# Two gated cross-attention blocks on one core: the first block's mixture moved to TensorE, and several pieces of work put elsewhere in the engines' orders

## The reference

```python
x = x + tanh(g_xattn[0]) * wkv(w, u, k=layernorm(x), v=ctx)
x = x + tanh(g_ffn[0])   * ffn(layernorm(x), w_gate_up, w_proj)
x = x + tanh(g_xattn[1]) * attention(layernorm(x), ctx, mask)
x = x + tanh(g_ffn[1])   * fp8_linear(layernorm(x), weight, bias)

# wkv: two scans over the 64 tokens of each batch row with the decay exp(w):
#   sums of exp(k) * v and of exp(k); y = (sum + exp(u+k) v) / (sum + exp(u+k))
# ffn: gate, up = x @ q(w_gate_up).T; h = silu(gate) * up; rms_norm(h) @ q(w_proj).T
#   q: each group of 64 weights becomes -s, 0 or +s, s the mean magnitude of the group
# fp8_linear: one scale from the greatest |x| of the whole tensor, x rounded to fp8
```

## Time and profile before

| | us |
|---|---|
| median of 3 runs (lowest, highest) | 138.73 (138.19, 139.01) |
| profiled execution | 137.42 |
| its span | 135.6 |
| mean granted TensorE clock of the span | 0.962 |
| TensorE busy | 115.7 |
| VectorE busy | 112.8 |
| ScalarE busy | 90.6 |
| GpSimd busy | 34.9 |

### The profile page before, as it was taken

One profiled execution on the slowest core, in us unless ns is written; L12 is line 12 of the kernel. 1 busy time (PEld: TensorE's weight loads), 2 busy tenths in 40 slices (PEclk: granted clock), 3 DMA queues, 4 the chain that ended last, 5 costly groups with the idle time before them and its releaser, 6 DMA issues.

```text
span 135.6 us, 2220 instructions
## 1 busy us (share of the span) xinstructions
PE 115.7 (85%) x729; PEld 76.4 (56%) x739; DVE 112.8 (83%) x265; ACT 90.6 (67%) x188; POOL 34.9 (26%) x79
## 2 busy tenths in 40 slices
PE   5958799960999799999987999999997768899991
PEld 5846674410523356477653676766666546677680
DVE  5999999998995979999986896938898897882970
ACT  2487789039584877685775777895975555864962
POOL 7917100006000000000134712019537432620000
PEclk9999999997557999999999999999999999999999
DMA  4999970000000000000000000000000000000035
GB/s 122 272 346 352 381 214 2 0 0 0 0 0 0 0 5 2 0 0 0 0 0 5 2 0 0 0 5 0 0 2 0 5 0 2 0 2 0 5 116 193
DMA packets 7110, 6.90 MB, mean 51 GB/s; under 512 B 1336, under 2 KB 6842, under 8 KB 7098
## 3 DMA queue, kind: packets, MB, share of 16 engines
q1 hardware_dynamic: 7088, 6.75, 15.7%
q10 hardware_dynamic: 10, 0.00, 0.0%
HBM read 5.70 MB, written 1.05 MB: 50 GB/s over the span
## 4 chain that ended last, share of the span: by engine, by line
PE 52%; DVE 16%; ACT 14%; DMA 7%; SPq 5%; issue 5%; DVEq 0%
PE ps L850 8%; PE ps L851 7%; DMA wgu_raw<-in_L_ffn_w_gate_up_dram 7%; PE ps L909 5%; DVE xs L1216 4%; PE ps L883 4%; PE ps L1103 4%; DVE stats L1127 3%; PE ps L770 3%; PE ps L772 3%; ACT xn L521 2%; PE ps L815 2%; ACT wT L527 2%; PE ps L752 2%; PE ps L841 2%
## 5 line engine op out<-in xcount | busy, mean ns | idle before, releaser
L850 PE MATMUL ps<-wT,xhi 128*128 128x512 bf16 x60 | 23.8, 396 | 1.3 <-ACT xlo L544 1.0
L851 PE MATMUL ps<-wT,xlo 128*128 128x512 bf16 x60 | 23.4, 390 | 0.2
L909 PE MATMUL ps<-wT,wgu_raw 128*128 128x256 bf16 x128 | 16.6, 273 | 0.1
L417 POOL TENSOR_SCALAR ve<-mv 128x2 f32<-128x2 f32 (+2 forms) x10 | 2.5, 246 | 52.8 <-DVE mv L1133 52.8
L909 PEld LDWEIGHTS ps<-wT,wgu_raw 128*128 128x128 f16 x128 | 12.4, 98 | 1.6 <-DVE wgu_raw L1283 0.3
L1127 DVE BATCH_NORM_STATS2 stats<-xs 128x6 f32<-128x256 f32 x32 | 12.3, 413 | 1.1 <-DMA xs<-in_x_dram 0.8
L585 ACT ACTIVATE wgu_raw<-ps 128x512 f16<-128x512 f32 x16 | 9.5, 595 | 4.5 <-PE ps L883 4.0
L533 ACT ACTIVATE wscale<-ps 128x1024 bf16<-128x1024 f32 x6 | 6.1, 1023 | 8.4 <-PE ps L772 8.4
L850 PEld LDWEIGHTS ps<-wT,xhi 128*128 128x128 f16 x64 | 6.4, 100 | 7.7 <-ACT xlo L544 1.5
L851 PEld LDWEIGHTS ps<-wT,xlo 128*128 128x128 f16 x64 | 6.5, 101 | 7.3 <-issue 1.1
L883 PE MATMUL ps<-ident,hbuf 128*128 128x128 f32 x64 | 9.7, 275 | 0.9 <-DVE wgu_raw L1283 0.9
(11 more groups left out here) (172 smaller groups left out, 282.8 us busy)
## 6 DMA issues: line engine op xcount, KB each, us to landing
wgu_raw<-in_L_ffn_w_gate_up_dram SPq DMA_DIRECT2D x4, 512.0 KB, 8.9
ctx_sb<-in_ctx_dram SPq DMA_DIRECT2D x2, 512.0 KB, 7.4
wp_raw<-in_L_ffn_w_proj_dram SPq DMA_DIRECT2D x1, 1024.0 KB, 10.1
out_dram<-xs SPq DMA_DIRECT2D x3, 256.0 KB, 2.1
xs<-in_x_dram SPq DMA_DIRECT2D x2, 256.0 KB, 3.0
xs<-in_x_dram SPq DMA_DIRECT2D x1, 512.0 KB, 6.9
wlin_raw<-in_L_ffn_weight_dram SPq DMA_DIRECT2D x1, 256.0 KB, 9.0
out_dram<-xs SPq DMA_DIRECT2D x2, 128.0 KB, 1.9
```

Of the source, the lines that this page charges most:

```text
L850: pe.matmul(ps[:, bank, :], xhi[:, h, c, o:o + P], w, start=(c == 0), stop=False)
L851: mm = pe.matmul(ps[:, bank, :], xlo[:, h, c, o:o + P], w, start=False, stop=(c == CH - 1))
L909: mm = pe.matmul(proj_at(i), part[:, n % 2, j * P:(j + 1) * P], wT[:, GU_PAIRS + f, j * C:(j + 1) * C], start=(first and f == 0 and j == 0 ...
```

## The change: what it does

- The first half's mixture is formed in PSUM: `mix_x` multiplies x with the identity into banks 0 and 1 (in place of six warm-up matmuls), `mix_y` adds y times tanh(g) times the identity (`ident_tg`, made by ScalarE at the start). ScalarE copies the banks to `res` (`mix_in`). `y_back(0)` and `mix_out` go.
- Variance plus epsilon and the shift of the first half are formed on VectorE, the root stays on GpSimd. ScalarE normalises all four tiles.
- GpSimd forms the two products of the second half (k = 2, 3) ahead of that root, after den_bonus(2). VectorE no longer does.
- `weight_rest` alternates between banks 6, 7 and 4, 5, so that (0) and (1) wait for no eviction. (0) to (3) are issued before the transposes, (4) in unit 0 and not in unit 1.
- gate(0) waits for the first low part alone; up(0) also for `gmax_done`, since the spread of the scales uses bank 1.
- VectorE's units: numerator scans 2 and 3 both in unit 3; bonus(3), both outputs and the quantisation of pair 5 in unit 4.
- project(6) is issued ahead of gate(8). The last unit's `hbuf` is turned in bank 1.
- Tail: `residual_back(2)` ahead of the third transposes, `spread_greatest` ahead of the last ones, no warm-up before it and two in place of four after it, `residual_back(4)` after the linear's block 1.
- The memset of `group_spread` goes from GpSimd to VectorE.

```diff
-WARM_LAST = 6
-WARM_TURN = 4
+WARM_TURN = 2
+    REST_BANK = [6, 4, 6, 4, 6, 6]
+        def turned(n):
+            return ps[:, 1 if n == UNITS - 1 else 3, :]
 # GpSimd
-            pool.memset(group_spread[:, :, :], 0.0).then_inc(spread_0, 1)
+            def wkv_product(k):
+                v = ctxT[:, k % CH, CT:NTOK].rearrange("p (b t) -> p b t", t=T)
+                pool.wait_ge(ctxT_ready, k + 1)
+                pool.wait_ge(G_ready, k + 1)
+                pool.tensor_tensor(kv[:, k, 1, :, 1:T + 1], kv[:, k, 0, :, 1:T + 1], v, ALU.mult).then_inc(GV_ready, 1)
             power(0, TPC, TPC, 2)
-            power_and_shift(1, 0, TPC, 1)
+            pool.wait_ge(den_ready, 3)
+            wkv_product(2)
+            wkv_product(3)
+            pool.wait_ge(ve_ready, 1)
+            pool.tensor_tensor(rstd[:, 1, 0:TPC], ve[:, 1, 0:TPC], minus_half[:, 0:TPC], ALU.pow).then_inc(rstd_ready[1], 1)
 # ScalarE
+            act.activation(ident_tg[:, :], ident[:, :], ACT.Copy, scale=tg[:, 0:1]).then_inc(ident_tg_ready, 1)
+            def mix_in(b):
+                act.wait_ge(mix_ps, b + 1)
+                act.activation(res[:, 2 * b:2 * b + 2, :]..., ps[:, b, :], ACT.Copy).then_inc(mix_ready, 1)
             invert(1)
+            mix_in(0)
+            mix_in(1)
+            invert(2)
             rest_in(0)
             rest_in(1)
-            invert(2)
-            ln_apply(1, 0, TPC // 2, 1)
+            act.wait_ge(mix_ready, 2)
+            ln_apply(1, 0, 2, 1)
+            ln_apply(1, 2, 2, 1)
 # TensorE
             def weight_rest(n):
-                    pe.wait_ge(rest_ready, n)
+                if n >= 2:
+                    pe.wait_ge(rest_ready, (0, 0, 1, 2, 3, 5)[n])
+            def mix_x():
+                pe.wait_ge(in_x[0], 16)
+                pe.wait_ge(in_x[1], 16)
+                pe.wait_ge(G_ready, CHUNKS * CH)
+                for i in range(TPC):
+                    o = (i % 2) * C
+                    pe.matmul(ps[:, i // 2, o:o + C], ident[:, :], xs[:, i, :], start=(i % 2 == 0), stop=False,
+                              skip_group_check=True)
+            def mix_y():
+                pe.wait_ge(y_ready, CH)
+                pe.wait_ge(ident_tg_ready, 1)
+                for i in range(TPC):
+                    for c in range(CH):
+                        o = (i % 2) * C + c * P
+                        mm = pe.matmul(ps[:, i // 2, o:o + P], y[:, c, i * P:(i + 1) * P], ident_tg[:, :], start=False,
+                                       stop=(i % 2 == 1 and c == CH - 1), skip_group_check=True)
+                    if i % 2:
+                        mm.then_inc(mix_ps, 1)
             def gate(n):
                 if n == 0:
-                    pe.wait_ge(G_ready, CHUNKS * CH)
+                    pe.wait_ge(mix_ready, 2)
+                    pe.wait_ge(mv_ready[1], 1)
+                    pe.wait_ge(xlo_ready, 1)
+                    pe.wait_ge(wq_ready, WQ_GATE[0])
+                if n == 2:
                     pe.wait_ge(xlo_ready, 2)
-                    pe.wait_ge(wq_ready, WQ_GATE[0])
             def up(n):
                 if n == 0:
                     pe.wait_ge(wq_ready, WQ_UP[0])
+                    pe.wait_ge(gmax_done, 1)
             def h_back(n):
-                if n >= 1:
+                if 1 <= n < UNITS - 1:
                     pe.wait_ge(hlo_ready, n)
-            keep_warm(WARM_FRONT, 0, wabs)
+            mix_x()
             for p in range(PAIRS):
                 weight_sums(p)
-            y_back(0)
-            weight_rest(0)
-            weight_rest(1)
+            mix_y()
+            for n in range(4):
+                weight_rest(n)
             spread_scales()
...
-            weight_rest(2)
             for n in range(UNITS + 2):
+                if n == 2 * TPC:
+                    project(n - 2)
                 if n < UNITS:
                     gate(n)
                     up(n)
...
                 if n == 0:
-                    weight_rest(3)
-                if n == 1:
                     weight_rest(4)
...
             channel_major(3, 1, xn3T_ps)
+            residual_back(2)
             channel_major(3, 2, xn3T_ps)
-            residual_back(2)
             channel_major(3, 3, xn3T_ps)
-            keep_warm(WARM_LAST, 7, wT)
+            spread_greatest()
             channel_major(3, 4, xn3T_ps)
-            spread_greatest()
             residual_back(3)
-            residual_back(4)
             keep_warm(WARM_TURN, 4, wT)
 # in the linear's loop, after block k
+                if k == 1:
+                    residual_back(4)
 # VectorE
+            dve.memset(group_spread[:, :, :], 0.0).then_inc(spread_0, 1)
             den_scan(2)
             weights_scale()
-            mix_out()
-            ln_stats(1, 0, TPC)
             den_bonus(2)
+            mix_stats()
             greatest_scales()
-            ln_apply(1, TPC // 2, TPC // 2, 1)
+            norm_shift()
             den_scan(3)
...
                 if n == 3:
-                    wkv_product(2)
-                    wkv_product(3)
                     num_scan(2)
+                    num_scan(3)
                     num_bonus(2)
+                if n == 4:
+                    num_bonus(3)
                     wkv_out(2)
-                if n == 4:
-                    num_scan(3)
-                    num_bonus(3)
                     wkv_out(3)
-                if n == 5:
                     quant_here(5)
                     quant_sign(5)
+                if n == 5:
                     mix_pair(2)
                     ln_stats(1, 4, 2)
```

More of the change, by code:

```diff
@@ L100, in gated_blocks @@
         neg_bf = sb("neg_bf", [P, P], BF16)
+        ident_tg = sb("ident_tg", [P, P])
         scales = sb("scales", [SCALE_ROWS, 512], BF16)
@@ L531, in rest_in @@
                 p = QUANT_ORDER[n]
+                bank = REST_BANK[n]
                 act.wait_ge(rest_ps, n + 1)
-                act.activation(wscale[:, p, :].rearrange("p (a b) -> p a b", a=2), ps[:, 6:8, :],
+                act.activation(wscale[:, p, :].rearrange("p (a b) -> p a b", a=2), ps[:, bank:bank + 2, :],
                                ACT.Copy).then_inc(rest_ready, 1)
+            def mix_in(b):
+                act.wait_ge(mix_ps, b + 1)
+                act.activation(res[:, 2 * b:2 * b + 2, :].rearrange("p i c -> p (i c)"), ps[:, b, :], ACT.Copy).then_inc(mix_ready, 1)
             def xn_high(k):
@@ L768, in weight_rest @@
                 for a in range(2):
-                    bank = 6 + a
+                    bank = REST_BANK[n] + a
                     pe.matmul(ps[:, bank, :], group_spread[:, SCALE_ROW[p] // 2 + a, :], scales[:, :],
@@ L894, in project @@
                 if n == 0:
-                    pe.wait_ge(gmax_done, 1)
+                    pe.wait_ge(rest_ready, 4)
                     pe.wait_ge(wT_ready, PAIRS)
@@ L1048, in _ @@
                     h_back(n - 1)
-                if n >= 2:
+                if n >= 2 and n != 2 * TPC:
                     project(n - 2)
@@ L1220, in residual, with mix_stats, norm_shift @@
                 dve.wait_ge(res_ready[stage], count)
-            def mix_out():
-                dve.wait_ge(tg_ready, 1)
-                dve.wait_ge(yT_ready, 2)
-                residual(1, 0, TPC, lambda i: ps[:, XN_BANKS[0][i // 2], (i % 2) * C:(i % 2 + 1) * C], lambda i: tg[:, 0:1], 1)
+            def mix_stats():
+                last = None
+                for i in range(TPC):
+                    if i % 2 == 0:
+                        dve.wait_ge(mix_ready, i // 2 + 1)
+                    now = step(dve.bn_stats(stats[:, i, :], res[:, i, :]))
+                    if i > 0:
+                        after(last)
+                        step(dve.bn_aggr(mv[:, 1, i - 1, :], stats[:, i - 1, :]))
+                    last = now
+                after(last)
+                dve.bn_aggr(mv[:, 1, TPC - 1, :], stats[:, TPC - 1, :]).then_inc(mv_ready[1], 1)
+                dve.wait_ge(mv_ready[1], 1)
+                dve.tensor_scalar(ve[:, 1, 0:TPC], mv[:, 1, 0:TPC, 1], LN_EPS, 1.0, ALU.add, ALU.mult).then_inc(ve_ready, 1)
+            def norm_shift():
+                dve.wait_ge(rstd_ready[1], 1)
+                dve.scalar_tensor_tensor(out=shift[:, 0:TPC], in0=mv[:, 1, 0:TPC, 0], scalar=-1.0, in1=rstd[:, 1, 0:TPC],
+                                         op0=ALU.mult, op1=ALU.mult).then_inc(shift_ready, 1)
             def mix_pair(k):
-                dve.wait_ge(yT_ready, k + 1)
-                residual(1, 2 * k, 2, lambda i: ps[:, XN_BANKS[1][k - 2], i * C:(i + 1) * C], lambda i: tg[:, 0:1], k)
+                dve.wait_ge(yT_ready, k - 1)
+                residual(1, 2 * k, 2, lambda i: ps[:, XN_BANKS[1][k - 2], i * C:(i + 1) * C], lambda i: tg[:, 0:1], k - 1)
             def weights_abs(p):
```

38 lines of the change are left out of this document (19 added, 19 removed).

## The result

| | median (lowest, highest), us | ratio to before, 95% interval |
|---|---|---|
| before, same chip | 138.66 (138.19, 139.01) | |
| after, first runs | 135.5 (134.14, 138.28) | 0.9692 [0.9635, 0.9749] |
| after, once more ("again") | 134.89 (134.11, 137.38) | 0.9717 [0.9693, 0.9741] |

What follows compares the result with a forecast made beforehand. No engine bounds the whole span; a chain of waits in four stretches does. Terms 2.7 - 1.7 + 0.5 + 0.55 + 0.6 = 2.65 us off the median 138.73 give 136.1 us, range 133.8 to 138.8.

Steps and rivals of the forecast that it cites:

- up to `ffn_in(2)`, low clock taken off: From the start to ffn_in(2): 2.7 us gained at full clock, 1.7 lost to a low spell, 1.0 left.
- project(6) ahead of gate(8): Unit 8: project(6) fills TensorE's 0.96 us wait for the low copy of x; 0.5 us gained.
- h_back(15) in bank 1: Start of the tail: the last h no longer waits for hlo(14); 0.55 us gained.
- the tail's end: Last linear: the greatest value's spread goes 1.4 us earlier, but TensorE's queue lets only 0.6 us arrive.
- VectorE's units 3 to 5: Pair 5's quantisation in unit 4 delays the sixth hbuf to 61.05, hidden by TensorE's queue; uncovered, up to 2.7 us.
- The front: Start, before ScalarE's exponentials: moved group_spread memset and new ident_tg copy cost 0, bounds -0.3 to +0.6 us.
- The first silu: Chain ahead of the loop: silu(0) starts at 39.35 us instead of 40.99, set by ScalarE's own queue.
- The clock: Low spell moves later, into the loop's start; a third of it, 3.4 us, is taken, costing 1.7 us.
- Long products: Rival: GpSimd's two products run long, VectorE's quantisations come 2.3 us late; 1.5 us more, 137.6. Chance 0.14.
- Chain not shortened: Rival: mix_y's weight loads or ScalarE's longer queue keep the first silu at 41; 138.8 us. Chance 0.11.
- The long spell in the dense loop: Rival: low clock starts at 41.9 and lasts 10.24 us in the loop; 0.75 us slower, 139.5. Chance 0.13.
- No spell: Rival: no low clock in the loop, so 4.35 us is gained; 134.4 us. Chance 0.22.

Runs made afterwards that it cites:

- old_tail: The changed kernel with the old tail, its old warm-up matmuls and the last h back in bank 3: 135.74 us, ratio 0.9808.
- f_proj: fill with project(6) back behind gate(8): 131.86 us, ratio 0.955.
- prod_dve: The changed kernel with the second half's two products back on VectorE in unit 3: 135.36 us, ratio 0.9707.
- fill: pad with eight unread matmuls of 512 columns between gate(0) and up(0): 132.69 us, ratio 0.9589.
- f_wr4: fill with weight_rest(4) back in unit 1: 131.64 us, ratio 0.952.
- old_units: fill with VectorE's old order in units 3 to 5, products still on GpSimd: 132.64 us, ratio 0.9613.
- no_mix: fill without the first half's mixture on TensorE; VectorE adds y to the residual in four instructions: 133.35 us, ratio 0.9646.
- pad: The changed kernel with the operands of the weight sums and of the scales' spread zero-padded from 24 to 128: 133.27 us, ratio 0.9591.
- best: fill with project(6) behind gate(8), weight_rest(4) in unit 1 and residual_back(4) ahead of the linear, replacing two unread matmuls: 130.35 us, ratio 0.9446.

## Why the prediction was right, and where its sum was not

**Direction and place: right.** The chain to the first silu got shorter, the gain reached the end, part of it went into a low clock inside the loop. That the sum came so near is in part luck: several of its terms were off, and they pull both ways. In "again" that spell lay at 41.5 to 44.9, 3.4 us long, in the end of `weight_rest(4)` and in gate(1) and up(1), inside the stretch of 38 to 46 that was forecast.

**The terms**, profiled executions, us gained:

| term | forecast | "again" against before |
|---|---|---|
| up to `ffn_in(2)`, low clock taken off | 1.0 | 1.74 |
| project(6) ahead of gate(8) | 0.5 | -0.35 |
| h_back(15) in bank 1 | 0.55 | 0.70 |
| the tail's end | 0.6 | 0.41 |
| sum | 2.65 | 2.50 (own time 2.41) |

The first row hides two opposite errors, in the front and in the clock, which are taken up below. The third and fourth are confirmed by "old_tail".

**project(6): the step that failed.** I filled TensorE's 0.96 wait for the low copy of x and did not ask what project(6) filled where it stood. Behind gate(8) and up(8) it ran while ScalarE made the high copy of h(7); with it gone TensorE waits 0.69 there (74.43 above). It also starts late itself, 0.47 for `hlo(6)`. "f_proj", with project(6) put back, has neither of these two waits, only the old 0.96, and gained 0.3 to 0.4.

**The loop's start: two pacemakers.** The forecast put the second `hbuf` 4.25 behind the first (44.25 and 40.0), because gate(1) stands behind `weight_rest(4)`'s wait. Two executions show just that, at full clock: silu(0) is late there, so is the eviction behind it, TensorE waits for it (1.64 and 2.49), and the second `hbuf` comes 4.12 behind the first. "old_tail", then "prod_dve":
```profile
44.52 0.75 DVE L1361 SCALAR_TENSOR_TENSOR hbuf<-ps,pscale,sil 128x512 f32<-128x512 f32 x1 [0.40 <-PE ps L900]
```
```profile
45.83 0.75 DVE L1358 SCALAR_TENSOR_TENSOR hbuf<-ps,pscale,sil 128x512 f32<-128x512 f32 x1 [0.40 <-PE ps L897]
```
From the first `hbuf` to `ffn_in(2)` both take 26.26, forecast 26.75 (40.0 to 66.75). Where up(0) comes last, as in "fill", the eviction is nearly done when TensorE asks for it, and VectorE sets the distance, 3.38 in "fill" and in "f_wr4" alike, up to the fourth `hbuf`. The move of `weight_rest(4)` cost even there, 0.3 by the times and 0.58 by the trace. In "fill" TensorE waits 0.25 ahead of it for the eviction (39.85 to 40.10) and 0.31 ahead of h_left(1) for the high copy (47.25 to 47.56); in "f_wr4" both are gone. The wait of 0.69 for the first high copy stands in both, so it wasn't that one that the old place filled.

**VectorE's units 3 to 5.** Counted as hidden; measured 0.6 gained ("old_units"). The forecast credited VectorE's earlier tile to the products it shed. They didn't matter ("prod_dve"): it was the order, with both scans and the quantisation ahead of the time when the tile is asked for ("old_units" waits 0.42 for it).

**The front: a term put at nothing.** The forecast took 0, with bounds of -0.3 to +0.6, for the moved memset and for `ident_tg`. In "again" VectorE's scan at the end of the front started 1.19 late (24.64 to 25.83), outside these bounds: the late transfer and `ident_tg` held up ScalarE's exponentials by 1.08 and 0.31, and 1.19 of it reached the scan. In "old_tail", "prod_dve" and "fill" it was 0.21, 0.52 and 0.58 late. The transfer's part changes from execution to execution: TensorE waited 1.01 for it in "fill" and not at all in before. The late front is the likely reason why the profiled pair differs by 2.4 us only, less than the medians.

**The first silu.** It came at 39.15, 39.35 was forecast; `mix_in` took 0.60 each, `mix_y` had its 16 records (26.19 to 28.17, a pace of 0.124; 0.12 was taken): right. The products took 1.16 each (1.17 forecast). The Trainium skill (SBUF — State Buffer, Who interferes with whom) says that VectorE work with at most one input from SBUF, outside the modes that use two ports, does not contend with GpSimd; 2.32 for two, beside the batch statistics, agrees. They began at 28.37 and not at 27.2, since den_bonus(2) was as late as the scan ahead of it. They ended at 30.69, and the root followed at 30.79 instead of 29.75. Where the front was nearly in time, the forecast's times came out: in "old_tail" the products began at 27.39 and the root at 29.87, released by `ve`:
```profile
27.39 2.32 POOL L434 TENSOR_TENSOR kv<-kv,ctxT 128x512 f32<-128x512 f32 x2 [14.54 <-DVE ratio L1233]
29.87 1.01 POOL L442 TENSOR_TENSOR rstd<-ve,minus_half 128x4 f32<-128x4 f32 x1 [0.16 <-DVE ve L1285]
```
In "again" the late shift (31.83, forecast 31.0) and with it the quantisations and `gmax_done` put up(0) at 39.60 (forecast 38.6) and the first `hbuf` at 40.73 (forecast 40.0); in "fill", whose shift was 0.61 earlier, the first `hbuf` came at 40.12.

**The clock: the size, not the mechanism.** In "again" `ffn_in(2)` stands 26.95 behind the first `hbuf`. At full clock it is 26.26 in "old_tail" and "prod_dve"; with VectorE setting the second `hbuf` it would be some 0.7 less, an estimate (4.12 less 3.38). So the spell cost 0.7 to 1.4, where 1.7 was taken. The forecast also charged the new order 1.7 us more for the clock than the old one. With both orders padded and filled:

| | as they were | padded and filled, full clock |
|---|---|---|
| order before | 138.0 to 138.7 | 135.3 |
| order after | 134.9 to 135.5 | 131.95 to 132.26 |
| difference | 3.2 and 3.7 | 3.0 to 3.4 |

The padding's faster matmuls are in both right-hand values, which are of two chips. The low clock and the 24 rows together cost each order about 3 us. So the moves themselves are worth 3.0 to 3.4, less than the 4.35 the forecast had at full clock (the missing 0.85 of project(6) would be most of it), and the clock took little or nothing more from the new order than from the old. The two errors partly cancelled: the moves were put some 1 us too high and the clock's share too high as well.

**The rivals.** Long products: refuted by 2.32 for two. Chain not shortened: refuted by 39.15, and by "no_mix", where the shift, the first `hbuf` and the end are all 1.0 later. The long spell in the dense loop: single executions came near it (138.28, with 32.4 to 39.2 and 46.0 to 49.4 low), the median didn't. No spell: never seen in the kernel as changed (eleven executions, none above 0.987); "pad" has none in two of six, and "f_wr4" in all of five. Two of the signs of being wrong, "a clock low past 46" and "a silu at 41", did occur in the first profile (46.0 to 49.4, and 42.58), without making that execution slower than the median of before.

**The tail.** The forecast said that TensorE's queue with `residual_back(4)` in it would be the end, and kept 0.6 of 1.4. Right: of the 1.23 gained at the greatest value behind h_back(15) (3.32 - 2.09), "again" kept 0.41, and "best", without `residual_back(4)` in the linear, has the 42 matmuls in one piece and gains 0.8.

What stays open: what starts a low spell in a given execution. Which of the three spells falls is different from one execution to the next of the same program. Open too is what in the padding keeps the clock up, the 128 rows and columns or the shorter matmuls, since "pad" changed both together.

## What to carry to other kernels

Before an instruction goes into a wait, look at what it fills where it stands: project(6) had filled TensorE's wait for the high copy of h, and `residual_back(4)` the wait ahead of the linear. Look as well at what stands behind the new place: `weight_rest(4)` brought a wait for an eviction ahead of gate(1). Putting the three back took the padded and filled kernel from 131.95 to 130.15 at full clock. Compare executions at the same granted clock before crediting a change: 3.4 us more at half clock came with 0.9 to 1.2 us in "fill". It isn't a fixed price, though: before, in that comparison, took 138.01 to 138.40 at 0.962 to 0.963 and 138.06 to 139.02 at 0.947 to 0.950. In a profiled execution, see first whether its front began in time. And try to pad short operands of TensorE with zeros where the memory allows it: a few lines gave 1.6 us here, half of what the moves gave.
